# Turning all four heads' probabilities with block transposes and SBUF-to-SBUF transfers in a fused attention kernel

## The reference

```python
q = rope(rmsnorm(x @ Wq.T)); k = rope(rmsnorm(x @ Wk.T)); v = x @ Wv.T   # 32 query heads, 8 key heads, size 128
for b in batches:                       # 8
    for g in key_heads:                 # 8, each with 4 query heads
        keys = concat(k_cache[pages[b], g], k[b, g])     # 512 cached + 128 new = 640 keys
        vals = concat(v_cache[pages[b], g], v[b, g])
        s = (q[b, 4g:4g+4] @ keys.T) * SCALE             # cached keys past the length are masked
        ctx = softmax(s) @ vals
out = ctx @ Wo.T + residual
```

## Time and profile before

| what | value |
|---|---|
| runs (3) | 1300.09 to 1301.01 us, median 1300.29 |
| profiled execution, span from the first to the last instruction | 1299.0 us |
| median of the runs less that span | 1.3 us |
| TensorE matmul | 96% of the span |
| VectorE, ScalarE, GpSimd | 76%, 64%, 64% |
| DMA queue q1 | 51.2% of 16 engines |

### The profile page before, as it was taken

One profiled execution on the slowest core, in us unless ns is written; L12 is line 12 of the kernel. 1 busy time (PEld: TensorE's weight loads), 2 busy tenths in 40 slices (PEclk: granted clock), 3 DMA queues, 4 the chain that ended last, 5 costly groups with the idle time before them and its releaser, 6 DMA issues. The chain is left out here.

```text
span 1299.0 us, 26260 instructions
## 1 busy us (share of the span) xinstructions
PE 1249.3 (96%) x7496; PEld 1074.6 (83%) x7496; DVE 985.6 (76%) x2388; ACT 837.8 (64%) x2505; POOL 836.1 (64%) x787
## 2 busy tenths in 40 slices
PE   5799997799999999999999999999999999999988
PEld 4677775688888888888888888888888888888878
DVE  3567857467888878887888778878888888788766
ACT  2667777466767676666766776676666767666731
POOL 1656656475767676758665876687667766775741
PEclk9899998899999999999999999999999999999999
DMA  7546554345455555555555555555555455455441
GB/s 264 204 170 243 206 217 151 104 115 146 133 139 134 140 140 142 143 139 134 146 136 146 137 144 131 139 137 144 134 143 140 131 143 143 126 138 141 134 133 65
DMA packets 288945, 191.48 MB, mean 147 GB/s; under 512 B 151201, under 2 KB 256674, under 8 KB 287778
## 3 DMA queue, kind: packets, MB, share of 16 engines
q1 hardware_dynamic: 287792, 189.64, 51.2%
q10 hardware_dynamic: 1010, 0.17, 0.1%
HBM read 143.60 MB, written 79.69 MB: 172 GB/s over the span
## 5 line engine op out<-in xcount | busy, mean ns | idle before, releaser
L1779 POOL TENSOR_TENSOR b_p_l<-b_moved,b_p_h 128x640 fp32r<-128x640 f32 x128 | 200.9, 1570 | 163.9 <-PE ps L1375 93.8
L1514 ACT ACTIVATE b_pf<-b_sm,b_mn 128x640 f32<-128x640 f32 x256 | 212.4, 830 | 127.5 <-DVE b_mn L1624 127.5
L1624 DVE CUSTOM_DVE_ANT_0 b_sm<-ps,mask_row,b_rstd 128x640 f32<-128x640 f32 x256 | 225.0, 879 | 53.7 <-PE ps L1301 48.8
L1526 ACT ACTIVATE b_p_h<-b_moved 128x640 fp32r<-128x640 f32 x128 | 94.7, 740 | 160.0 <-DMA b_moved<-blocks_of_probs 158.8
L1660 DVE SCALAR_TENSOR_TENSOR b_hacc<-ps,b_ri,b_hacc 128x512 f32<-128x512 f32 x248 | 182.4, 736 | 4.6 <-PE ps L1301 4.3
L1299 PE MATMUL ps<-b_w_h,x1t_h 128*128 128x512 f32 (+1 forms) x512 | 178.8, 349 | 0.1
L1299 PE MATMUL ps<-b_kt_h,b_qt_h 128*128 128x320 f32 x512 | 169.5, 331 | 4.6 <-DVE b_mn L1624 4.2
L1300 PE MATMUL ps<-b_w_l,x1t_h 128*128 128x512 f32 (+1 forms) x512 | 173.4, 339 | 0.0
L1301 PE MATMUL ps<-b_w_h,x1t_l 128*128 128x512 f32 (+1 forms) x512 | 173.2, 338 | 0.0
L1301 PE MATMUL ps<-b_kt_h,b_qt_l 128*128 128x320 f32 x512 | 159.3, 311 | 0.0
L1300 PE MATMUL ps<-b_kt_l,b_qt_h 128*128 128x320 f32 x512 | 159.2, 311 | 0.0
(11 more groups left out here) (177 smaller groups left out, 3371.1 us busy)
## 6 DMA issues: line engine op xcount, KB each, us to landing
blocks_of_probs<-b_blk SPq DMA_DIRECT2D x128, 320.0 KB, 2.4
b_moved<-blocks_of_probs SPq DMA_DIRECT2D x512, 80.0 KB, 2.1
kv_of_batch<-in_kv SPq DMA_DIRECT2D x128, 256.0 KB
b_ck<-kv_of_batch SPq DMA_DIRECT2D x64, 256.0 KB, 4.0
b_cv<-kv_of_batch SPq DMA_DIRECT2D x256, 64.0 KB, 1.9
raw<-in_w SPq DMA_DIRECT2D x32, 384.0 KB, 3.2
raw<-in_wo SPq DMA_DIRECT2D x32, 256.0 KB, 2.8
a_xt<-in_xt SPq DMA_DIRECT2D x8, 256.0 KB, 6.7
```

The costliest lines, as they stand in the source:

```text
L1514: act.activation(pf[:, h % 2], sm[:, h % 2], ACT.Exp, bias=mn[:, m.b % 2, h:h + 1], scale=-1.0, accum_out=rs[:, m.b % 2, h:h + 1]).then_in ...
L1526: act.activation(blocks_of(p_h[:, :, h * P:(h + 1) * P]), moved[:, d].rearrange("p (a t j) -> p a t j", a=LT, j=QUAD), ACT.Copy).then_inc( ...
L1624: dve.tensor_tensor_reduce(sm[:, h % 2], score_row, mask_row[:, m.b], rstd[:, m.b % 4, h:h + 1], -MASKED, ALU.add, ALU.min, mn[:, m.b % 2, ...
L1779: pool.tensor_tensor(blocks_of(p_l[:, :, h * P:(h + 1) * P]), moved[:, d].rearrange("p (a t j) -> p a t j", a=LT, j=QUAD), blocks_of(p_h[: ...
```

## The change

- `turn_probs`, `low` and the pair `blocks_away`/`blocks_back` go. All four heads take one way: `turn_blocks` on VectorE, `blocks_across` on SP (four transfers of 80 KB from `blk` in SBUF to `moved` in SBUF, each reading 32 partitions and writing all 128), `high` on ScalarE, `low_probs` on GpSimd. `blk` keeps two buffers, `moved` has four.
- Key n of a page group now stands on another partition (4j + c instead of 32c + j), so the value rows are loaded with a stride of four partitions and the columns of the new keys are reordered in `new_keys` (`by_block`).
- Scores use two pairs of banks (0 and 1, 2 and 3), so `scores(m, h)` waits for `minima` of head h - 2.
- `rope_keys` leaves GpSimd: its sum goes to VectorE (`key_sum`), its scaling to ScalarE (`turned_key`).
- SP's order per slot: head 0, head 1, key rows, chunk, head 2, head 3, value rows.
- `accumulate(before, 3)` moves ahead of `minima(m, 2)`. `low_probs(last, 3)` and `high(last, 3)` run early in the next slot.
- To make room in SBUF, `squares_out` becomes bf16 and small tiles of `phase3` share one tile; its waits for `pl_sb` go.

```diff
@@ -44,8 +44,6 @@
 EPS = 1e-6
 FOUR = 4
 LAST = B - 1
-BY_DMA = (0, 1)
-BY_PE = (2, 3)
 QUAD = 32
 MASKED = -1e30
 TWO_PI = (6.28125, 0.0019350051879882812, 3.019916050e-07)
...
@@ -1127,7 +1118,7 @@
         sb = lambda n, s, d=F32: ctx.enter_context(nc.sbuf_tensor("b_" + n, s, d))
         sem = lambda n: ctx.enter_context(nc.semaphore("b_" + n))
         (sync_first, tensor_first, scalar_first, vector_first, gpsimd_first), (xl_sb, x1_out) = first_stage
-        SC, PT, OT, SM, PJQ, PJK = 0, 2, 4, 5, 6, 7
+        SC, OT, SM, PJQ, PJK = (0, 2), 4, 5, 6, 7
         OUT = (SM, OT, OT, SM)
         NK = NT * P
...
@@ -1153,29 +1146,29 @@
         o_h, o_l = sb("o_h", [P, REP * P], F32R), sb("o_l", [P, REP * P], F32R)
         wo_h, wo_l = sb("wo_h", [P, REP, D], F32R), sb("wo_l", [P, REP, D], F32R)
         hacc = sb("hacc", [P, B, D])
-        blk = sb("blk", [P, len(BY_DMA), NK])
-        moved = sb("moved", [P, len(BY_DMA), NK])
...
 
         block = ctx.enter_context(nc.Block())
...
-                    sp.dma_start(cv[q * PSIZE:(q + 1) * PSIZE], rows_of).then_inc(cv_in, 16)
-
-            def blocks_away(m, h):
-
-                d = BY_DMA.index(h)
-                sp.wait_ge(blk_sb, len(BY_DMA) * m.n + d + 1)
-                wait(sp, moved_in[d], 16 * LT * m.n)
-                sp.dma_start(blocks_dram[d], blk[:, d]).then_inc(blk_out[d], 16)
-
-            def blocks_back(m, h):
-
-                d = BY_DMA.index(h)
-                sp.wait_ge(blk_out[d], 16 * (m.n + 1))
-                wait(sp, ml_sb, len(BY_DMA) * (m.n - 1) + d + 1)
-                for c in range(LT):
-                    rows_of = blocks_dram[d].rearrange("(a i) (c n) -> c i a n", a=LT, c=LT)[c]
-                    sp.dma_start(moved[c * QUAD:(c + 1) * QUAD, d].rearrange("p (a n) -> p a n", a=LT), rows_of).then_inc(moved_in[d], 16)
+                    sp.dma_start(cv[q::LT], rows_of).then_inc(cv_in, 16)
+
+            def blocks_across(m, h):
+
+                sp.wait_ge(blk_sb, REP * m.n + h + 1)
+                wait(sp, ml_sb, REP * (m.n - 1) + h + 1)
+                for a in range(LT):
+                    width = NK // LT
+                    sp.dma_start(moved[:, h, a * width:(a + 1) * width], blk[a * QUAD:(a + 1) * QUAD, h % 2]).then_inc(moved_in[h], 16)
 
             def slot(m, one, two, last):
-                if m:
-                    blocks_away(m, 0)
-                    blocks_back(m, 0)
-                    blocks_away(m, 1)
+                blocks_across(m, 0)
+                blocks_across(m, 1)
                 if two:
                     key_rows(two)
-                blocks_back(m, 1)
-                if two:
-                    value_rows(two)
                 if m.b in (2, 3, 4, 5):
                     chunk(m.g + 1, m.b - 2)
                 if m.b in (6, 7) and m.g + 1 < G:
@@ -1276,6 +1258,10 @@
                 if m.b == 0 and m.g > 0:
                     chunk(m.g, KT + 2)
                     chunk(m.g, KT + 3)
+                blocks_across(m, 2)
+                blocks_across(m, 3)
+                if two:
+                    value_rows(two)
 
             def rows(m):
...
-                for bank, place, keys in ((SC, slice(LEAD, 512), slice(0, CUT)), (SC + 1, slice(0, CUT), slice(CUT, NK))):
+                first = SC[h % 2]
+                for bank, place, keys in ((first, slice(LEAD, 512), slice(0, CUT)), (first + 1, slice(0, CUT), slice(CUT, NK))):
                     mm = three(ps[:, bank, place], (qt_h[:, k, q], qt_l[:, k, q]), (kt_h[:, k, keys], kt_l[:, k, keys]))
                 mm.then_inc(sc_ps, 1)
 
-            def turn_probs(m, h):
-                pe.wait_ge(exp_sb, REP * m.n + h + 1)
-                wait(pe, pl_sb, len(BY_PE) * m.n + BY_PE.index(h))
-                for i in range(NT):
-                    mm = pe.transpose(turned_row[:, i], pf[:, h % 2, i * P:(i + 1) * P], ident[:])
-                mm.then_inc(pt_ps, 1)
-
             def value_pairs(m):
 
                 k = m.b % 2
...
                 wait(pe, h_sb, REP * m.n - 1)
                 pe.wait_ge(vcl_sb, m.n + 1)
-                pe.wait_ge(ph_sb, len(BY_PE) * (m.n + 1))
-                pe.wait_ge(mh_sb, len(BY_DMA) * (m.n + 1))
+                pe.wait_ge(mh_sb, REP * (m.n + 1))
                 for h, l, i in value_pairs(m):
                     pe.matmul(ps[:, OT, :], h, p_h[:, i], start=i == 0, stop=False)
...
-                turn_probs(m, 2)
                 if two:
                     project_q(two)
...
 
+            def turned_key(m):
+                act.wait_ge(kab2_sb, m.n + 1)
+                act.wait_ge(rstd_sb, m.n + 1)
+                act.activation(ka[:], kb[:], ACT.Copy, scale=rstd[:, m.b % 4, REP:REP + 1]).then_inc(kr_sb, 1)
+
...
-                    wait(act, blk_sb, len(BY_DMA) * m.n + turned_by_dve(h - 2))
-                    wait(act, pt_ps, len(BY_PE) * m.n + turned_by_pe(h - 2))
+                wait(act, blk_sb, REP * m.n + h - 1)
                 if h == 0:
                     wait(act, ri_sb, m.n - 1)
                 act.activation(pf[:, h % 2], sm[:, h % 2], ACT.Exp, bias=mn[:, m.b % 2, h:h + 1],
                                scale=-1.0, accum_out=rs[:, m.b % 2, h:h + 1]).then_inc(exp_sb, 1)
 
             def high(m, h):
-                act.wait_ge(pt_ps, len(BY_PE) * m.n + BY_PE.index(h) + 1)
+                act.wait_ge(moved_in[h], 16 * LT * (m.n + 1))
                 wait(act, pvh_ps, m.n)
-                act.activation(p_h[:, :, h * P:(h + 1) * P], turned_row, ACT.Copy).then_inc(ph_sb, 1)
-
-            def high_moved(m, h):
-                d = BY_DMA.index(h)
-                act.wait_ge(moved_in[d], 16 * LT * (m.n + 1))
-                wait(act, pvh_ps, m.n)
-                act.activation(blocks_of(p_h[:, :, h * P:(h + 1) * P]), moved[:, d].rearrange("p (a t j) -> p a t j", a=LT, j=QUAD),
+                act.activation(blocks_of(p_h[:, :, h * P:(h + 1) * P]), moved[:, h].rearrange("p (a t j) -> p a t j", a=LT, j=QUAD),
                                ACT.Copy).then_inc(mh_sb, 1)
 
...
                     kv_weights(m.g + 1)
-                high_moved(m, 0)
+                high(m, 0)
+                if one:
+                    turned_key(one)
                 if last:
                     output(last)
                 exponent(m, 3)
-                high(m, 2)
+                high(m, 1)
                 if one:
                     new_keys(one)
                     cache_values(one)
-                high_moved(m, 1)
+                high(m, 2)
                 if m.n == end.n - 1:
                     h_out(act, 0)
...
 
+            def key_sum(m):
+                dve.wait_ge(kab_sb, m.n + 1)
+                dve.tensor_tensor(kb[:], ka[:], kb[:], ALU.add).then_inc(kab2_sb, 1)
+
             def queries(m):
                 dve.wait_ge(qth_sb, m.n + 1)
                 dve.tensor_tensor(qt_l[:, m.b % 2], ps[:, PJQ, :], qt_h[:, m.b % 2], ALU.subtract).then_inc(qtl_sb, 1)
 
             def new_keys(m):
                 dve.wait_ge(knh_sb, m.n + 1)
-                dve.tensor_tensor(kt_l[:, m.b % 2, L:], ps[:, PJK, 0:P], kt_h[:, m.b % 2, L:], ALU.subtract).then_inc(knl_sb, 1)
+                by_row = lambda tile: tile[:, m.b % 2, L:].rearrange("p (c j) -> p c j", c=LT)
+                dve.tensor_tensor(by_row(kt_l), by_block(ps[:, PJK, 0:P]), by_row(kt_h), ALU.subtract).then_inc(knl_sb, 1)
 
             def minima(m, h):
...
 
-                d = BY_DMA.index(h)
-                if m.n == 0:
+                if m.n == 0 and h == 0:
                     dve.wait_ge(x1_out, 16 * B)
                 dve.wait_ge(exp_sb, REP * m.n + h + 1)
-                wait(dve, blk_out[d], 16 * m.n)
-                dve.transpose(by_quadrant(blk[:, d]), by_tile(pf[:, h % 2])).then_inc(blk_sb, 1)
-
-            def low(m, h):
-                dve.wait_ge(ph_sb, len(BY_PE) * m.n + BY_PE.index(h) + 1)
-                wait(dve, pv_ps, m.n)
-                cols = slice(h * P, (h + 1) * P)
-                dve.tensor_tensor(p_l[:, :, cols], turned_row, p_h[:, :, cols], ALU.subtract).then_inc(pl_sb, 1)
+                if h < 2:
+                    wait(dve, moved_in[h + 2], 16 * LT * m.n)
+                else:
+                    dve.wait_ge(moved_in[h - 2], 16 * LT * (m.n + 1))
+                dve.transpose(by_quadrant(blk[:, h % 2]), by_tile(pf[:, h % 2])).then_inc(blk_sb, 1)
 
             def output(m):
...
-                if last:
-                    low(last, 3)
+                if before:
+                    accumulate(before, 3)
                 minima(m, 2)
                 turn_blocks(m, 1)
-                if before:
-                    accumulate(before, 3)
+                if one:
+                    key_sum(one)
                 if m.n == end.n:
                     h_rest(dve, 1)
                 if one:
                     queries(one)
                 minima(m, 3)
+                turn_blocks(m, 2)
                 if last:
```

(26 more changed lines are left out.)

79 lines of the change are left out of this document (33 added, 46 removed).

## The result

| | before | changed |
|---|---|---|
| median, 4 runs each | 1300.19 us | **1406.3 us** (1398.9 to 1410.9) |
| ratio of the medians | 1 | 1.080, 95% interval 1.076 to 1.084 |
| span of the profiled execution | 1299.0 us | 1406.9 us |
| start of the first to start of the last `exponent(m, 0)`, 63 slots | 990.4 us | 1096.1 us |

The change makes the kernel 8% slower. Of the 107.9 us that the span grew, 105.7 lie between the first and the last `exponent(m, 0)`. The forecast was slower, 1318, and its range ended at 1345.

The account below looks back on a forecast made before the run. TensorE, always busy, bounds the kernel at 15.66 us a slot; after the change a chain round all engines through head 2's blocks does. +2.9 us per group, eight groups 23, less 5, plus 1.3 for the median: 1318 us, range 1258 to 1345.

Parts of the forecast that it names:

- The term that failed: SP's queue in one slot: four issues take 1.74 us, key rows 0.43, then a chunk; head 2's four start at E + 8.9.
- E: Start of `exponent(m, 0)` on ScalarE, the zero point from which the forecast times one slot's chain.
- the landing: Head 2's blocks from SP's issue at E + 8.9 to ScalarE's start at E + 14.0, behind key rows and chunk.
- The path that failed with it: Head 2's arrival summed as E + 8.05 (issue), then data terms 1.1, 1.45, 1.35, 1.6 and 0.5, making E + 14.0.
- The slots: Forecast slot lengths for the eight batches of a head group, 14.6 to 17.8 less 0.3, sum 128.2 against 125.3 us before.
- b: Batch number, 0 to 7, of a slot; a slot is one batch of one head group in the attention stage.
- TensorE's floor: TensorE's issue time per slot without the transposes: 14.64 us, down from 15.66.
- Rival 1: SP's queue does not matter: head 2 lands 3.28 us after its own issue, most slots 14.64, total 1264; chance 0.27.
- Rival 3: SP stalls on issue as well: four issues sometimes take 2.60 us instead of 1.74, total 1345; chance 0.16.
- Rival 4: VectorE's key sum waits for a GpSimd instruction; b = 1 and 6 grow about 1 us, total 1334; chance 0.08.
- The signs I named: Idle TensorE before `values_of_highs`, ScalarE waiting for head 2's blocks, b = 6, 0, 5 longest, SP waiting for weights in b = 6.

Follow-up runs that it names:

- run 2: Changed kernel, each head still four 80 KB transfers but from 32 partitions to the same 32, rows of 2560 bytes (keys mixed); 1397.9 us.
- run 3: Changed kernel, four 80 KB transfers a head, each a quarter of the columns from 128 partitions to the same 128 (keys mixed); 1376.0 us.
- run 12: run 1 plus three tiny, unneeded SBUF-to-SBUF transfers a head (16 bytes from each of 32 partitions) ahead of the 320 KB one; 1424.5 us.
- run 1: Changed kernel with one 320 KB transfer a head, 128 partitions to the same 128, instead of four of 80 KB (keys mixed); 1269.1 us.
- run 5: Changed kernel with SP's order turned: all four heads' blocks, then key rows, value rows and the chunk last; 1313.8 us.
- run 9: Changed kernel with the single transfers of run 1 and the turned SP order of run 5 together (keys mixed); 1254.4 us.
- run 6: Changed kernel with head 2's `high` and `low_probs` moved into the next slot and head 1's a little later; SP's order kept; 1308.4 us.
- run 15: Changed kernel with two 160 KB transfers a head, 64 partitions to the same 64, instead of four of 80 KB (keys mixed); 1336.7 us.
- run 4: Kernel before with only the value rows strided to every fourth partition, still from DRAM; 1305.6 us beside 1299.1.
- run 13: run 10 with ScalarE's four value-row issues set apart, each behind a long activation; 1277.3 us, ratio 0.982 to the kernel before.
- run 10: run 5 with the four value-row transfers issued by ScalarE behind its copy of the queries instead of by SP; 1286.7 us, ratio 0.988.
- run 8: Changed kernel with the edits of run 5 and run 6, each head's blocks going through DRAM, one transfer out and one back; 1515.7 us, ratio 1.167.

## Why the prediction was wrong in size and right in direction

- **The term that failed**: "SP issues four transfers in 1.74, to E + 8.05, then the key rows (0.43, E + 8.5), then a weight chunk ..., then head 2's four from E + 8.9." From one issue of the new kind to the next it takes 0.65 us, not 0.43, for 512 bytes as for 80 KB (runs 2, 3, 12). Head 1's four end at E + 8.57, key rows and chunk take 1.9 us instead of 0.85, head 2 starts 1.58 late. From the earlier trace rows, which read from DRAM, I took a duration for a transfer between two places in SBUF and gave it no range, while I gave one to the landing. The chunk was mis-sized in the same way, 0.43 against 1.13 here (median 1.25). In the kernel before it took 0.43 in 29 of 32 slots, but not in the very slot that the forecast was read from:

```profile
814.23 1.56 SPq L1230 DMA_DIRECT2D raw<-in_w  x1
```

- **The path that failed with it**: in the sum the issue time enters once (1.74), and from the key rows' issue on the data carries it (1.1 + 1.45 + 1.35 + 1.6 + 0.5). In the slot above the issues carry it: the last of head 2's four starts at 451.53, E + 12.39, and lands 2.48 us later, E + 14.87, which is when ScalarE's `high` starts (14.90). Of the data terms the block transfers were read too short besides: the forecast's own windows of 167 and 179 GB/s make 1.96 and 1.83 us of 320 KB, not 1.6.
- **The landing** (5.1 from head 2's first issue to ScalarE) was too dear: 4.42. Of the 1.58 late 0.7 came back; with 0.06 less on ScalarE's last steps 0.84 is left, 16.54 against 15.70.
- **The slots**: the medians for b = 0 to 7 are 18.0, 16.0, 16.7, 16.9, 16.8, 18.0, 18.3 and 16.5, sum 137.1. I had 17.1, 14.6, 15.7 three times, 16.7, 17.5, 15.2, sum 128.2. The pattern is right and each entry is 0.8 to 1.4 short; b = 1, where I gave TensorE's floor, is bound by the same chain. 8.9 a group is 71 of the 88 us between 1318 and 1406.
- **The other 17 us** are mostly single slots 1 to 2 us over their median, which I had not counted. In the slot from 298.57 head 2's last issue starts at 311.16 and ScalarE goes on at 315.32, 4.16 us later; in between the DMA share falls to 0.07:

```profile
313.00:313.75 0.75, 0.75 (x8) 0.75 (x7) 0.51 (x1) 0.00 (x0) 0.75 (x1) 1.00 0.46 120
313.75:314.50 0.75, 0.75 (x5) 0.65 (x4) 0.00 (x0) 0.00 (x0) 0.11 (x1) 1.00 0.07 10
```

  One of 16 engines is then at work, on 640-byte pieces of the blocks. Just ahead of that, from 312.00 to 313.60, a 16 KB packet of the instruction queue was under way. It is the place of such a packet that goes with the length, not how many a slot has: where one is under way between E + 11 and E + 15, when head 2's blocks are crossing, the slot is on average 0.98 us over the median of its b (22 slots); the other 41, with a packet elsewhere or none, are 0.13 under it. In b = 3 the three such slots take 18.4 to 18.5 us and the other five 16.4 to 17.1. 22 x 0.98 is more than the 17 us. In run 1, where TensorE binds, the 22 slots with a packet in the same place are only 0.15 over. It fits that a fetch of instructions on one DMA engine holds up that engine's share of the block transfer; no run took it away, so it is not shown.
- **Rival 1** ("the queue does not matter") was wrong: head 2 lands 4.42 after its first issue, not 3.28, and turning the order alone is worth 92 us (run 5). **Rival 3** (SP stalls on issue as well, 1345) had the right mechanism at a third of its size (27 us over 1318 where 88 were missing); it had it as an exception that "sometimes" occurs. Its condition, a landing past E + 13.0, is met at 14.90. **The floor** (14.64) is borne out: in run 9, 35 slots stand at 14.5 to 14.7.
- **Rival 4** (`key_sum` blocks): it happens, and in this change costs next to nothing. 17 of 64 instances took over 0.35 us, all 64 together 25.0 us instead of 15.7. The longest took 1.38 us, 1.1 too long, and head 2's transposes end a median of 1.88 us before SP comes to issue them, so in most slots there is room for it. An instance alone and one beside GpSimd's `kt_l` (829.98 to 831.28):

```profile
812.77 0.25 DVE L1578 TENSOR_TENSOR b_kb<-b_ka,b_kb 128x128 f32<-128x128 f32 x1
```

```profile
830.70 0.74 DVE L1578 TENSOR_TENSOR b_kb<-b_ka,b_kb 128x128 f32<-128x128 f32 x1
...
831.36 0.68 DVE L1582 TENSOR_TENSOR b_qt_l<-ps,b_qt_h 128x512 fp32r<-128x512 f32 x1
```

  The Trainium skill (SBUF — State Buffer, "Who interferes with whom") says that a VectorE instruction with two SBUF inputs contends with a GpSimd instruction that reads SBUF; the trace agrees, at 0.25 against 0.74 us here and a mean of 1.02 in run 6.
- **The signs I named** for "right" were all there: TensorE idle before `values_of_highs`, put down to the accumulate; ScalarE's longest wait for the moved blocks of head 2 (224.9 of its 286.2 us); b = 6, 0 and 5 the longest slots; SP's wait for the weights' remainder in b = 6 (13.9 us in 7 slots). They mark the chain, and did not tell its data from its issues.
- The Trainium skill (DMA: Bandwidth & Descriptors, "Issuing engines are not separate DMA queues") holds that issuing from several engines saves only the time it takes to initiate a transfer, usually small relative to the transfer. Here that time is 0.65 us against a landing of 2.2 and, times 22, it makes 14.3 us of a slot: moving four issues to ScalarE and hiding them there was worth 36 us (1313.8 to 1277.3).

## What to carry to other kernels

Count a queue's issues like an engine's instructions: number times the distance between two, taken from rows with the same source, the same destination partitions and the same transfer ahead of them, and where there is no such row give that distance a range of its own. Then lay the queue's order on the critical chain: the same issues cost 92 us more when loads with time to spare stand ahead of a transfer that a chain waits for. If a queue is full, issue the leisurely transfers from another engine, one at a time, each right behind a long instruction of that engine.

## What the hardware showed that I had not expected

- The distance between two issues on SP: 0.47 us (median; 0.34 at the least) for DRAM into 32 neighbouring partitions, 0.65 for DRAM into every fourth partition, 0.63 to 0.65 for SBUF to SBUF in four shapes from 512 bytes to 80 KB, but 0.56 for 160 KB between 64 partitions and for 320 KB between 128 (runs 15 and 1). What in the transfer sets it was not separated further.
- The transfer ahead has a part in it. The unchanged key rows take 0.43 us to issue behind a transfer from SBUF to DRAM and 0.59 behind one from SBUF to SBUF; the unchanged 384 KB chunk 0.43 behind value rows into neighbouring partitions, 0.59 behind strided ones, 1.25 behind key rows (medians; before and run 4, the change, run 5).
- An issue on ScalarE's queue (0.58 us) runs beside the activation ahead of it and then costs ScalarE next to nothing (4.0 us in all, run 13); four in a row cost about 1.9 us each time (100.8 in 54 slots, run 10).
- A round trip through DRAM took 7.2 us from the first issue to ScalarE in run 8's slot, one way from SBUF to SBUF 3.9 to 5.0 in those of run 1, the change and run 15.
